# Turning the first two chunks of passes 4 and 5 at other points of a lane's order

## Time and profile before

| | |
|---|---|
| median of 3 runs | 1260.37 us (1260.17 to 1260.38) |
| profiled execution | 1260.2 us |
| its span, first to last instruction | 1258.2 us |
| TensorE busy | 1228.9 us, 98% |
| VectorE busy | 758.8 us, 60% |
| ScalarE busy | 215.5 us, 17% |
| POOL busy | 62.0 us, 5% |
| mean granted TensorE clock | 0.996 |

### The profile page before, as it was taken

One profiled execution on the slowest core, in us unless ns is written; L12 is line 12 of the kernel. 1 busy time (PEld: TensorE's weight loads), 2 busy tenths in 40 slices (PEclk: granted clock), 3 DMA queues, 4 the chain that ended last, 5 costly groups with the idle time before them and its releaser, 6 DMA issues.

```text
span 1258.2 us, 16358 instructions
## 1 busy us (share of the span) xinstructions
PE 1228.9 (98%) x5872; PEld 1028.3 (82%) x5872; DVE 758.8 (60%) x1863; ACT 215.5 (17%) x392; POOL 62.0 (5%) x52
## 2 busy tenths in 40 slices
PE   8999999999999999999999999999999999999996
PEld 6888888788878887878888888878888888888875
DVE  5836897787776777778635554462246255544624
ACT  5622111121111101120111111020111111110110
POOL 0000000000000000000000001010000000010100
PEclk9999999999999999999999999999999999999998
DMA  9832112211111110101011032033001111320320
GB/s 342 327 101 60 38 49 65 72 45 39 52 55 55 47 38 24 44 22 43 15 34 34 20 90 64 13 105 80 1 27 42 34 34 28 86 64 9 95 58 36
DMA packets 128646, 78.16 MB, mean 62 GB/s; under 512 B 97312, under 2 KB 108064, under 8 KB 126752
## 3 DMA queue, kind: packets, MB, share of 16 engines
q1 hardware_dynamic: 128560, 77.05, 21.1%
HBM read 53.42 MB, written 23.59 MB: 61 GB/s over the span
## 4 chain that ended last, share of the span: by engine, by line
PE 90%; DVE 6%; DMA 2%; issue 1%; SPq 1%; ACT 1%; DVEq 0%; ACTq 0%
PE ps L672 29%; PE ps L673 29%; PE ps L776 20%; PE ps L690 8%; PE ps L711 2%; PE ps L712 2%; DVE nat L1038 1%; DVE ring L1038 1%; DMA raw<-in_at 1%; PE ps L684 1%; DVE xs L936 1%; DVE sml L980 0%; SPq L1080 0%; ACT xs L810 0%; DVE sml L971 0%
## 5 line engine op out<-in xcount | busy, mean ns | idle before, releaser
L672 PE MATMUL ps<-B,xs 128*128 128x512 f32 x1664 | 654.9, 394 | 4.2 <-DVE xs L936 4.2
L673 PE MATMUL ps<-B,xs 128*128 128x512 f32 x1664 | 648.0, 389 | 0.0
L672 PEld LDWEIGHTS ps<-B,xs 128*128 128x128 f32 x1664 | 312.6, 188 | 67.9 <-ACT xs L810 3.9
L673 PEld LDWEIGHTS ps<-B,xs 128*128 128x128 f32 x1664 | 312.7, 188 | 62.3
L776 PE MATMUL ps<-Tw,xs 128*128 128x512 f32 x1280 | 309.3, 391 | 2.5 <-DVE ring L1038 2.5
L776 PEld LDWEIGHTS ps<-Tw,xs 128*128 128x128 f32 x1280 | 238.6, 188 | 55.1 <-DVE ring L1038 4.6
L924 DVE TENSOR_TENSOR ring<-ps,rrep 128x512 f32<-128x512 f32 x94 | 64.5, 689 | 252.7 <-PE ps L673 244.2
L1038 DVE SCALAR_TENSOR_TENSOR nat<-ps,embn,nat 128x128 f32<-128x128 f32 x448 | 153.6, 343 | 51.1 <-PE ps L776 50.8
L1038 DVE SCALAR_TENSOR_TENSOR ring<-ps,embn,ring 128x128 f32<-128x128 f32 x512 | 175.0, 342 | 0.0
L690 PEld LDWEIGHTS ps<-W,ring 128*128 128x128 f32 x896 | 111.5, 191 | 12.0 <-DVE ring L924 3.7
L690 PE MATMUL ps<-W,ring 128*128 128x128 f32 x896 | 113.2, 275 | 4.4 <-DVE ring L924 2.5
(11 more groups left out here) (66 smaller groups left out, 542.9 us busy)
## 6 DMA issues: line engine op xcount, KB each, us to landing
raw<-in_at SPq DMA_DIRECT2D x13, 1024.0 KB, 16.2
td<-ring SPq DMA_DIRECT2D x32, 256.0 KB, 2.0
ring<-td SPq DMA_DIRECT2D x128, 64.0 KB, 2.5
ring<-in_xn SPq DMA_DIRECT2D x16, 256.0 KB, 2.9
ring_x<-in_xt SPq DMA_DIRECT2D x32, 128.0 KB, 3.2
ring_x<-y1d SPq DMA_DIRECT2D x32, 128.0 KB, 3.2
out<-nat SPq DMA_DIRECT2D x16, 256.0 KB, 2.3
y1d<-ring SPq DMA_DIRECT2D x14, 256.0 KB, 2.8
```

The source lines that it names most:

```text
L672: pe.matmul(bank, x[:, 0, m, :], of, start=m == 0, stop=False)
L673: mm = pe.matmul(bank, x[:, 1, m, :], of, start=False, stop=ends and m == NT - 1)
```

## The change

The turn of chunk 0 leaves `one_pass` and stands in `second`, behind the previous pass; its back stands in front of the splits. The turn of chunk 1 goes in front of the first quarter instead of the third, and its back in front of the second instead of the fourth. Chunks 2 and 3 stay.

```
@@ one_pass
         for c, m in order:
             if p == 2 and j < 2 and (c, m) == (0, 2):
                 put("split", j, 2, 3)
-            if p in (4, 5) and (c, m) == (0, 0):
-                turn(0, 0)
-            if p in (4, 5) and (c, m) == (0, 1):
-                put("back", j, p, 0, 0)
-            if p in (4, 5) and c < 3 and m == 2:
+            if p in (4, 5) and c < 3 and m == (2 if c else 0):
                 turn(c + 1, 0)
-            if p in (4, 5) and c < 3 and m == 3:
+            if p in (4, 5) and c < 3 and m == (3 if c else 1):
                 put("back", j, p, c + 1, 0)
@@ second
         for p in (4, 5, 6):
+            if p < 6:
+                put("turn", j, p, 0, 0)
             yield
+            if p < 6:
+                put("back", j, p, 0, 0)
             splits(j, p)
             yield
```

## The result

| | before | after |
|---|---|---|
| median of 20 runs each, same chip | 1261.49 us (1260.17 to 1263.31) | 1258.22 us (1256.88 to 1261.03) |
| ratio | | 0.9973, 95% interval 0.9967 to 0.9979 |
| profiled execution | 1260.2 us | 1260.51 us |
| its span | 1258.2 us | 1258.6 us |
| mean granted clock of that execution | 0.996 | 0.993 |

The change gains 3.3 us, 0.27% (2.6 to 4.2 us by the interval). The forecast of 1.96 us has the right sign and is too small: 1258.22 lies in the range, but the gain is beyond the 2.5 us that I had taken for distinguishable, and I had given "faster" 0.06. That 1258.22 stands only 0.2 us from the forecast time of 1258.4 is luck: the forecast started from the 1260.37 us of three runs, 1.1 us under the median of twenty, and its gain was 1.3 us too small.

The account below looks back on a forecast made before the run. TensorE was taken as the bound, busy 1228.9 of 1258.2 us. Gains of 2.02 and 0.28 less 0.34 make 1.96 us, taking the 1260.37 us median to 1258.4; range for 8 in 10: 1258.0 to 1260.1.

Parts of the forecast that it names:

- faster: Whole kernel: a gain beyond the 2.5 us that a measurement can tell from no change; chance 0.06, from E.
- The first hole: TensorE at 840.66, before the mix of pass 5's first chunk, waiting for a DMA back: closing it gains 2.02 us.
- The second hole: The same mix in the other odd pair, at 1182.62: closing it gains 0.28 us.
- The tight places: Pass 5 of the odd pairs: the moved transpose delays VectorE's scale, costing TensorE 0.17 us in each of two places, 0.34.
- Nothing given back: TensorE from 860 to 1160 us has no hole, so nothing there gives the gained time back.
- POOL's add: Chunk 0's bias add starts earlier, at about 823, among VectorE's splits and norms; nothing reaches TensorE, cost taken as 0.
- C: POOL's early add holds six VectorE instructions before chunk 1's turn, 1.3 us each; slower, 1261.0 us; chance 0.03.
- E: Whole kernel: gain larger than the holes, 2.5 us or more, though TensorE has only 2.30 to give; chance 0.06.

Follow-up runs that it names:

- filled_again: Same kernel as filled (before, plus eight unread products in pair 3's pass 5 hole), timed in one round for a second trace: 1261.92 us, ratio 1.0005.
- reload_later: The kernel before, with the reloads of pair 0's first two chunks issued later in SP's queue: 1259.99 us, ratio 0.9984.
- behind_splits: The changed kernel with the turn of chunk 0 behind the splits, one lane step later: 1256.93 us, ratio 0.9965 to before.
- c0_only: The changed kernel with chunk 1's turn and way back left at their old places: 1257.51 us, ratio 0.9969 to before.
- other_six: The kernel before with the change everywhere but in pass 5 of pairs 3 and 1: 1261.52 us, ratio 0.9998.
- filled: The kernel before with eight products that nobody reads in pair 3's hole of pass 5: 1262.5 us, ratio 1.0006.
- late_tfill: behind_splits with seven products that nobody reads in TensorE's hole at 563 us: 1257.39 us, ratio 0.9969 to before.
- three_holes: The changed kernel with three TensorE holes of about 2 us made on purpose at 898, 950 and 987 us: 1270.4 us, ratio 1.0067 to before.

## Why the prediction was right in its steps and short in its size

In the pair of first traces the three terms of the sum can be read from how far TensorE's rows stand apart in the two: 2.05, 0.32 and 0.25 us for 2.02, 0.28 and 0.34. That is 2.12 of the 2.20 us between the lanes, so for these two executions the sum was right. What failed is below.

- **The first hole, 2.02 us.** Closed as said: turn right behind the norm (820.28, on a time axis that is 2.8 us later), landed long before the mix. The size for the median was the error. It was read from one execution, which had 1.89 us of idle time in the two holes together; three others have 2.45, 2.15 and 2.21, and filled_again some 4.2 with its fill of 1.8 counted. What was taken as a property of the kernel is a draw from a spread: the turn's DMA took 3.64 to 3.82 us in five traces and 4.51 in a sixth, and TensorE could start 1.87 to 2.16 us behind the last DMA of the way back, where I had used 1.98.
- **The second hole, 0.28 us.** Closed as said; its idle row, 0.08 us in the first trace, was 0.16 to 0.44 in four other traces of kernels that have it, none in reload_later, and 1.69 in filled_again.
- **The tight places, 0.34 us.** At 822 (after: 825.17) TensorE starts 0.06 us behind the scale's end and lasts 1.16 us, both as worked out. TensorE's rows there moved by 0.12 us and by 0.13 at 1166, where I had 0.17 each. No idle row stands there, although I had said that one would; the start and the length show the wait, and in behind_splits, which pushes nothing in front of the scale, the length is back at 1.05.
- **Nothing given back.** Right: 300.00 of 300.00 busy between 860 and 1160. c0_only shows that chunk 1's part costs and gives nothing, other_six that the six other places don't either.
- **POOL's add.** I took 0 at the end, and that was right. VectorE is held, but TensorE needs none of what waits behind it so soon. The split that meets the add lasts 1.78 us instead of 0.69, once in each of the eight places (8.3 us more of VectorE in all), and the adds there 1.47 to 1.50 instead of 1.29. By the Trainium skill, "SBUF — State Buffer", section "Who interferes with whom", the second of two such instructions to issue waits for the first. The trace agrees in that VectorE is held once in each place, by 1.09 us. That is less than the whole length of the add, which I had put down for it, as the add is issued while the split ahead of the held one still runs. C fell with it: one split is held, not six instructions.
- **E, the step that failed.** I wrote of E that 2.5 us or more would need something that I don't see, "as TensorE has only 2.30 to give". That is a statement about one execution's idle rows, used as a bound on a median. Two things were outside of it: longer holes in other executions (some 0.4 us, by the 2.40 at the higher clock and by the other traces), and the lower clocks that go with the holes (an estimate of 1.1 us by the table). The earlier trace rows show a clock of 1.00 in all four stretches, from which I concluded that nothing was to be won; it says only that this execution lost nothing there.

**What stays open.** Where the lower clocks of before's runs lie isn't shown. The made holes show the mechanism, the count shows that the clocks go with the holes, and no trace joins the two: none of the four traces with the real hole at 841 shows half clock behind it. If 0.7 of the executions had a stretch there, four traces without one would come up once in a hundred times (0.3 to the fourth). That speaks against the account, unless the traced executions are not like the others. There is a sign of that: of the six traces of kernels without the holes five have a stretch at 23 to 25 or at 564 to 566 us, while of the 53 other runs of these kernels 30 have 0.997, so none at all. reload_later, whose hole is half as long, has low clocks as often, which speaks against the account too, unless its low clocks lie elsewhere, as those of its own trace do (at 23 and 566 us). filled, whose share is 4 of 20, speaks for it. Why filled's DMAs land late more often isn't settled.

The holes at 23 and 564 us are in all kernels (but for late_tfill, which fills the second). Of 14 traces seven show half clock at 23 to 25 us and four at 564 to 566, of either kind of kernel. Nothing ahead of the lanes was changed, so I took that part for spread and no gain; it is not measured on its own.

## What to carry to other kernels

A hole that ends on a DMA has a length that belongs to one execution; take it from several, or widen the range upward by what the landing varies (here by 0.9 us in the first place and 1.4 in the second, most of it from one execution). A gap in TensorE costs more than its idle row when the clock falls behind it in part of the executions: 1.6 us each time in this kernel. Closing the two real gaps won half as much again as their idle time, and the profiled execution did not show it. Compare stretches between two fixed idle rows rather than spans when a half-clock stretch lies elsewhere.

## What the runs showed of the hardware

- Behind holes of 1.8 to 2.3 us TensorE's clock was at the lower level for 3.41 us in part of the cases (in three_holes behind 1.96 and 2.23 us, not behind 2.29), at a price of 1.6 us. It began between 0.15 us before TensorE resumed (reload_later, at 23.32) and 1.5 us after (after, at 566.30).
- A VectorE subtraction of 128x512 from SBUF beside a POOL add on SBUF took 1.78 us instead of 0.69, and the add 1.50 instead of 1.29; one meeting, one hold.
- The same DMA of 256 KB to DRAM landed in 2.25 us with no reload issued shortly ahead of it (2.21 to 2.25 in six traces at the second mix), in 3.64 to 3.82 with two ahead, and in one execution, that of filled_again, in 4.51 and 3.57.
